# Two scatters of rows, and who signals the end of a matmul: matmul or drain

## The chip, the cores and the metric

The kernel runs on one core of a Trainium2 chip. The metric is the time of one execution on the device in microseconds (us). The core's engines are PE (TensorE, matmuls), DVE (VectorE), ACT (ScalarE), POOL (GpSimd) and SP (SyncE, which here only issues transfers). Each runs its own list of instructions in order; they meet at semaphores, which one instruction increments when it ends and another waits for.

## What is computed

Two layers over x of 16 x 256 x 128. Layer 0 multiplies a gated linear attention ("gla", a recurrence over chunks of 64 tokens with 4 heads) by the silu of a mixture of 8 experts; layer 1 multiplies a causal softmax attention with 16 heads by the silu of a mixture of 16 experts. Each token goes to its 2 best experts.

```python
xn = _layernorm(x)
s = _L0_attn_ref(xn, ...)            # gated linear attention
g = _silu(_L0_ffn_ref(xn, ...))      # top 2 of 8 experts
x = x + s * g
xn = _layernorm(x)
s = _L1_attn_ref(xn, ...)            # causal softmax attention, 16 heads of 8
g = _silu(_L1_ffn_ref(xn, ...))      # top 2 of 16 experts
x = x + s * g
```

## The kernel before, in words

The 4096 tokens are 16 batches of 256. For each layer DVE works out (`route`) a slot for each of the 8192 pairs of token and expert; POOL then sends the normalised rows to their slots in DRAM (the scatter); SP reads the sorted rows back in groups of 512, PE runs them through the experts (`ffn0` with 18 groups, `ffn1` with 20), and POOL stores the results with indirect transfers of its own (L1710).

One function, `walk`, fixes the order in which all engines write their programs. The parts that matter here:

- Layer 0: after `route(0)` come six turns t = 1 to 6. In each, POOL issues about a sixth of 64 indirect transfers of 128 rows (`scatter(0, t - 1, 6)`, L1694), and all engines do `gla(t, 0)`, `gla(t, 1)`, `gla(t, 2)`, one turn of the attention's software pipeline: gates (L430), keys times values (L481), turned keys (L456), scores (L469), values (L447), outputs (L495, L502), queries and keys (L441), projection (L516). Between its transfers POOL does two small steps of each turn: `output_gates` (L1730), which waits for ACT, and `chunk_ends` (L1724), which waits for ACT's exponentials; ACT's next exponentials wait for `chunk_ends`. Then `ffn0_begin` turns the first group of rows (L557), and the next turn of gla follows with the experts between its parts.
- Layer 1: after `route(1)` come seven turns in which POOL issues its 64 transfers with nothing between them but four small copies (L1690), while PE, ACT and DVE do 18 steps of the softmax attention ("mha", five steps to a batch of 256 tokens: 3.6 batches), and ACT and DVE also convert a piece of the expert weights (`mf`, L870 and L1353) in each turn. Then `ffn1_begin` turns the first group (L557 again), which needs the scatter done.

In an mha step `s1_four` makes four banks of scores (L679, closed by L682), which DVE reduces to maxima (L1580); `s2_four` makes four banks of scores turned the other way (L702, L706, closed by L709), of which ACT takes exponentials (L1110); `weigh` (L721, L723) multiplies by the values, `outputs_turned` (L748) and `heads_out` (L734) turn the results, and `queries_keys1` (L656) makes the next batch's queries and keys. PE hands out eight PSUM banks in a ring: a bank comes free when the engine that reads it has signalled.

In each of these steps the last matmul of a group carries the semaphore update for the reader, as `i.then_inc(qk.sem, 1)`; in `s1_four` and `s2_four` each of the four closing matmuls carries one. On PE `scatter` does nothing; it is only a point in the walk. The names `scattering`, `ended`, `scatter` and `begin` in the change are PE's alone.

Of the kernel before, what the change touches and what calls it, by code (L numbers as in the profile page):

```python
# [51 lines left out]
def build(nc, A, out):  # L52
    with ExitStack() as ctx:
# [26 lines left out]
        xnT = sb(4096)  # L80
# [262 lines left out]
        def _(eng):  # L343
# [10 lines left out]

            mm = partial(eng.matmul, start=True, stop=True, skip_group_check=True)

            def expert_logits(l, g):
                h, E = due(l, LOGITS, g), EXPERTS[l]
                if h is not None:
                    u = 8 * l + h  # L360
                    b = bank(("logits", u), l_moved.at(u))
                    eng.wait_ge(*n_moved.at(u))
                    if h == 0:
                        eng.wait_ge(*ld[f"rw{l}"].at(0))
                    for k in range(4):
                        t = 4 * h + k
                        i = mm(b[:, E * k:E * k + E], xnT[:, 128 * t:128 * t + 128], rw[l])  # L367
                    i.then_inc(logits.sem, 1)
                    if l == 0:
                        b = bank(("silu", h), silu_done.at(h))  # L370
                        if h == 0:
                            eng.wait_ge(*ld["wvg"].at(0))
                        mm(b[:, :], Wvg[:, 128:256], xnT[:, 512 * h:512 * h + 512]).then_inc(silu.sem, 1)

            def normed_turned(l, g):
                h = due(l, TURN, g)
                if h is not None:
                    u = 8 * l + h
                    b = bank(("norm", u), n_moved.at(u))
                    eng.wait_ge(*normed.at(u))  # L380
                    if u == 0:
                        eng.wait_ge(*ld["cst"].at(0))
                    for k in range(4):
                        i = eng.transpose(b[:, 128 * k:128 * k + 128], xn[:, 4 * h + k, :], ident)
                    i.then_inc(n_turned.sem, 1)

# [9 lines left out]
            def route(l):  # L396
                N, O = 64 * EXPERTS[l], one_hot[:, 0:64 * EXPERTS[l]]
                nh = N // 2
                eng.wait_ge(*chosen[l].at(1))
                eng.wait_ge(*set_dve.at(0, 3))  # L400
                for n, lhs in enumerate((trib, onesb)):
                    for i in range(2):
                        b = bank(("count", l, n, i), counts.at(l, 2 * n + i))
                        mm(b[:, 0:nh], lhs, O[:, nh * i:nh * i + nh]).then_inc(counted.sem, 1)
                if l == 1:
                    b = bank(("table", l), routed[l].at(0, 22))
                    eng.wait_ge(*routed[l].at(0, 21))
                    eng.wait_ge(*ld["phase"].at(0))
                    for c in range(2):
                        i = mm(b[:, 80 * c:80 * c + 80], phe[0:16, 128 * c:128 * c + 128], RS[l]["oh"][0:16, :])  # L410
                    i.then_inc(tabled.sem, 1)


            def gate_in(b):
                k = bank(("gate1", b), gate1_lo.at(b))
                if b == 0:
                    eng.wait_ge(*ld["gk1"].at(0))
                mm(k[0:80, 0:256], Wgk1, xnT[:, 256 * b:256 * b + 256]).then_inc(gate1.sem, 1)

            def gate_out(b):  # L420
                G = g1T[b % 2]
                eng.wait_ge(*gate1_lo.at(b))
                if b == 0:
                    eng.wait_ge(*set_dve.at(0, 3))
                for hp, k in enumerate(gate_banks):
                    if b > 0:
                        eng.wait_ge(*decay.at(b - 1, hp))
                    for h in range(2):
                        hh = 2 * hp + h
                        i = mm(k[:, 256 * h:256 * h + 256], Wgk2b[0:82, 128 * hh:128 * hh + 128], G[0:82, :])  # L430
                    i.then_inc(gate2.sem, 1)
# [12 lines left out]
            def values(b):  # L444
                k = bank(("v", b), v_moved.at(b))
                for u in range(2):
                    i = mm(k[:, 128 * u:128 * u + 128], xnT[:, 256 * b + 128 * u:256 * b + 128 * u + 128], Wvg[:, 0:128])  # L447
                i.then_inc(vv.sem, 1)

            def keys_turned(b, u):  # L450
# [4 lines left out]
                for h in range(4):  # L455
                    i = eng.transpose(k[:, 128 * h:128 * h + 128], k4[:, h, 128 * u:128 * u + 128], ident)  # L456
                i.then_inc(kt.sem, 1)

            def scores(b):
# [10 lines left out]
                i.then_inc(att.sem, 1)  # L470

            def key_values(b):
# [9 lines left out]
                i.then_inc(kv.sem, 1)  # L482

            def outputs(b):
# [12 lines left out]
                for n in range(1, 4):  # L497
# [5 lines left out]
                    if n > 1:  # L503
                        i.then_inc(o_mm.sem, 1)

            def output_means(b):
                eng.wait_ge(*o_sq.at(b))
                mm(o_banks[0][:, 256:512], means, osq[b % 2]).then_inc(o_mean.sem, 1)

            def project(b):  # L510
# [4 lines left out]
                for u in range(2):  # L515
                    i = mm(k[:, 128 * u:128 * u + 128], oy[b % 2][:, 128 * u:128 * u + 128], Wo)  # L516
                i.then_inc(wo_mm.sem, 1)

# [33 lines left out]
            def turn(l, g):  # L552
# [3 lines left out]
                for j in range(4):  # L556
                    i = eng.transpose(k[:, 128 * j:128 * j + 128], xsb[:, 129 * j:129 * j + 128], ident)  # L557
                i.then_inc(turned[l].sem, 1)
                if g == 0:
# [11 lines left out]
            def expert_up(l, g, j):  # L571
# [17 lines left out]
                for c in range(4):  # L589
# [6 lines left out]
                    if l == 0:  # L596
                        i = mm(o, b1r[:, 128 * c:128 * c + 128], b1s[:, bass.DynSlice(v * 128, 128)], start=False)  # L597
                i.then_inc(up[l].sem, 1)

# [46 lines left out]
            def queries_keys1(b, half):  # L646

                for n in (2 * half, 2 * half + 1):
# [8 lines left out]
                    j.then_inc(m_qk.sem, 1)  # L657

            def values1(b):
# [4 lines left out]
                for u in range(2):  # L664
                    i = mm(k[:, 128 * u:128 * u + 128], xnT[:, 256 * b + 128 * u:256 * b + 128 * u + 128], Wv)
                i.then_inc(m_v.sem, 1)

            def s1_four(b, n):
# [11 lines left out]
                for i, k in four:  # L680
                    kv_ = k[:, :].rearrange("p (n c) -> p n c", c=w)
                    mm(kv_[:, :, w - 128:w], identb, bc(negb, 1, [128, len(gs), 128]), start=False).then_inc(m_s1.sem, 1)  # L682

            def maxima_turned(b):
                k = bank(("neg", b), m_neg_moved.at(b))
                eng.wait_ge(*m_max.at(b))
                for u in range(2):
                    i = eng.transpose(k[:, :].bitcast(BF16)[:, 128 * u:128 * u + 128], negM[b % 2][:, u, :], identb)
                i.then_inc(m_neg.sem, 1)

            def s2_four(b, n):
# [15 lines left out]
                for i, k in four:  # L707
                    kv_ = k[:, :].rearrange("p (n c) -> p n c", c=w)
                    mm(kv_[:, :, 0:128], identb, bc(negtb, 1, [128, len(gs), 128]), start=False).then_inc(m_s2.sem, 1)  # L709

            def weigh(b, z):
# [6 lines left out]
                for m in range(2):  # L718
# [3 lines left out]
                    for i in range(4):  # L722
                        j = mm(k[32 * i:32 * i + 32, 256 * m + 128:256 * m + 256], V[:, 1, 4 * g + i, :], PT[1][:, i, g, :], start=False)  # L723
                j.then_inc(m_pv.sem, 1)

            def outputs_turned(b):
                for u in range(2):
# [7 lines left out]
                    i.then_inc(m_ot.sem, 1)  # L735

            def heads_out(b):
                k = bank(("yt", b), m_yt_moved.at(b))
                eng.wait_ge(*m_y.at(b))
                for u in range(2):  # L740
                    i = eng.transpose(k[:, 128 * u:128 * u + 128], yt[:, 128 * u:128 * u + 128], ident)
                i.then_inc(m_yt.sem, 1)

            def project1(b):
                k = bank(("proj", b), s1_done.at(b))
                eng.wait_ge(*m_yt_moved.at(b))
                for u in range(2):
                    i = mm(k[:, 128 * u:128 * u + 128], yT[:, 128 * u:128 * u + 128], Wproj)  # L748
                i.then_inc(m_proj.sem, 1)

# [1205 lines left out]
```

## Time and profile before

| | us |
|---|---|
| median of 3 runs | 1166.89 (1165.84 to 1169.87) |
| the profiled execution | 1174.48 |
| its span, first to last instruction | 1172.5 |
| PE busy | 794.8 (68%) |
| DVE busy | 646.4 (55%) |
| ACT busy | 625.9 (53%) |
| POOL busy | 479.5 (41%) |
| mean granted TensorE clock | 0.83 |

The profile page gives the busy time of each engine, the span in 40 slices, and the chain of waits: the work that ended last, followed back from the end through whatever released each step. "issue" is time in which an engine waited for nothing that the profile shows; "another core or an unknown queue", and "remote" in the table of waits, is a wait for which the profile finds no event that ended it at that time. A matmul's end is modelled; its start is recorded.

### The profile page before, as it was taken

Reading aid. Unit: us, or ns where it says so; the run is one execution under the profiler, and the core shown is the slowest. Engines: PE = TensorE matmul, PEld = TensorE weight load, DVE = VectorE, ACT = ScalarE, POOL = GpSimd, SP = SyncE. Lnnn points to the kernel's source line nnn. Section 1 sums busy time; section 2 is a strip of 40 time slices with the busy share of each in tenths; the row PEclk is TensorE's granted clock in tenths of the full one; section 3 lists DMA queues with packets and bytes.
Section 4 is the critical chain, followed back from the end, with each engine's and each line's share of the span. In section 5 each row is a group of like instructions: output and inputs, shape, how many; then the busy total and the mean of one; then the engine's idle time right before and its main releaser. Section 6 shows DMA issues by size and latency. Waiting matters only on the chain.

```text
span 1172.5 us, 23626 instructions
## 1 busy us (share of the span) xinstructions
PE 794.8 (68%) x8916; PEld 620.2 (53%) x8916; DVE 646.4 (55%) x1112; ACT 625.9 (53%) x1093; POOL 479.5 (41%) x486
## 2 busy tenths in 40 slices
PE   5735668999999882477821028777988788788610
PEld 3424557888888762254610015455656566666510
DVE  7574336766765233977670016755656647465355
ACT  4433336768775311464500025667668778687722
POOL 3067542233432444520037730004346646555635
PEclk9667869999999997677955559989889999899855
DMA  9511111011011113300013111201001111010052
GB/s 325 190 45 55 52 39 45 21 34 34 29 34 33 47 47 111 78 1 2 1 29 147 52 43 37 73 19 29 20 28 38 35 31 38 28 38 29 19 152 72
DMA packets 62366, 63.92 MB, mean 55 GB/s; under 512 B 7378, under 2 KB 52322, under 8 KB 62132
## 3 DMA queue, kind: packets, MB, share of 16 engines
q1 hardware_dynamic: 53300, 43.99, 12.8%
q0 software_dynamic: 8960, 18.43, 4.8%
q8 instruction: 77, 1.26, 0.5%
q14 instruction: 29, 0.24, 0.1%
HBM read 31.84 MB, written 30.55 MB: 53 GB/s over the span
## 4 chain that ended last, share of the span: by engine, by line
PE 38%; DVE 19%; ACT 13%; another core or an unknown queue 11%; issue 10%; POOL 6%; DMA 2%; SPq 0%; POOLq 0%; ACTq 0%; DVEq 0%
PE bank L441 5%; POOL ys L1710 4%; PE bank L656 3%; ACT arena L1110 3%; PE bank L593 3%; DVE arena L1580 2%; ACT L804 2%; PE bank L595 2%; PE bank L607 2%; PE bank L481 2%; PE bank L594 2%; PE bank L721 2%; PE bank L621 1%; PE bank L367 1%
## 5 line engine op out<-in xcount | busy, mean ns | idle before, releaser
L1710 POOL DMA_INDIRECT ys<-arena x152 | 169.8, 1117 | 203.3 <-DVE arena L1472 86.0
L1110 ACT ACTIVATE arena<-bank 128x512 f32<-128x512 f32 x192 | 99.3, 600 | 137.2 <-remote 92.1
L1694 POOL DMA_INDIRECT xs<-arena x128 | 128.4, 1003 | 62.4 <-issue 36.5
L593 PE MATMUL bank<-arena 128*128 128x128 bf16 x608 | 139.2, 236 | 19.4 <-DVE arena L1453 7.4
L595 PE MATMUL bank<-arena 128*128 128x128 bf16 x608 | 138.8, 235 | 3.8 <-issue 3.8
L1580 DVE TENSOR_REDUCE arena<-bank 128x2 bf16<-128x512 f32 (+1 forms) x192 | 119.2, 683 | 40.2 <-remote 26.2
L594 PE MATMUL bank<-arena 128*128 128x128 bf16 x608 | 136.7, 232 | 3.9 <-issue 3.9
L804 ACT ACT_TABLE_LOAD x70 | 89.8, 1283 | 1.2
L593 PEld LDWEIGHTS bank<-arena 128*128 x608 | 63.3, 104 | 37.5 <-issue 28.5
L441 PE MATMUL bank<-arena 128*128 128x256 f32 x256 | 69.1, 424 | 18.4 <-DVE arena L1359 17.2
L679 PE MATMUL bank<-arena 32*128 32x256 bf16 (+1 forms) x512 | 22.3, 263 | 86.7 <-ACT arena L1110 61.2
L1750 POOL TENSOR_TENSOR arena<-arena 128x1024 f32<-128x1024 f32 x20 | 47.0, 2351 | 71.3 <-ACT arena L1025 71.2
L1500 DVE TENSOR_SCALAR arena<-bank 128x512 f32<-128x512 f32 x40 | 27.6, 691 | 85.5 <-ACT arena L1011 85.3
L1568 DVE SCALAR_TENSOR_TENSOR arena<-arena,bank 128x512 bf16<-128x512 bf16 x64 | 46.2, 746 | 47.4 <-ACT arena L1083 46.1
L441 PEld LDWEIGHTS bank<-arena 128*128 128x128 f32 x256 | 53.2, 216 | 29.5 <-DVE arena L1359 18.0
L595 PEld LDWEIGHTS bank<-arena 128*128 x608 | 62.8, 103 | 9.1 <-issue 4.3
L656 PE MATMUL bank<-arena 128*128 128x256 f32 x256 | 66.0, 404 | 0.7 <-issue 0.7
L594 PEld LDWEIGHTS bank<-arena 128*128 x608 | 63.8, 105 | 4.8 <-issue 4.4
L597 PE MATMUL bank<-arena 128*128 x288 | 63.3, 220 | 3.1 <-issue 3.0
L679 PEld LDWEIGHTS bank<-arena 32*128 32x128 bf16 x512 | 9.5, 96 | 97.1 <-issue 75.9
L1462 DVE SCALAR_TENSOR_TENSOR arena<-arena,bank 128x512 f32<-128x512 f32 x36 | 24.7, 690 | 54.8 <-ACT arena L987 35.0
L656 PEld LDWEIGHTS bank<-arena 128*128 128x128 f32 x256 | 49.5, 204 | 8.8 <-issue 2.5
(213 smaller groups left out, 2034.5 us busy)
## 6 DMA issues: line engine op xcount, KB each, us to landing
xs<-arena SPq DMA_DIRECT2D x19, 516.0 KB, 7.7
arena<-xs SPq DMA_DIRECT2D x38, 258.0 KB, 2.8
arena<-ys SPq DMA_DIRECT2D x32, 256.0 KB, 5.2
arena<-in_MF SPq DMA_DIRECT2D x8, 512.0 KB
ys<-arena POOLq DMA_INDIRECT x152
arena<-in_x SPq DMA_DIRECT2D x8, 256.0 KB, 5.6
arena<-in_W SPq DMA_DIRECT2D x8, 256.0 KB
xs<-arena POOLq DMA_INDIRECT x128
```

The source lines that it names most:

```text
L441: i = mm(k[:, 256 * h:256 * h + 256], (Wq, Wk)[n // 2][:, 128 * hh:128 * hh + 128], xnT[:, cols])
L593: mm(o, hi, b[:, 0, c4], stop=False)
L594: mm(o, hi, b[:, 1, c4], start=False, stop=False)
L595: i = mm(o, lo, b[:, 0, c4], start=False, stop=(l == 1))
L597: i = mm(o, b1r[:, 128 * c:128 * c + 128], b1s[:, bass.DynSlice(v * 128, 128)], start=False)
L656: j = mm(k[:, 256 * z:256 * z + 256], Wqk[:, c:c + 128], xnT[:, 256 * b:256 * b + 256])
L804: eng.preload_act_table_set(name)
L1110: act(PT[kt_][:, i, gs[0]:gs[0] + len(gs), :], bank_of["s2", b, n, i][:, :].rearrange("p (g q) -> p g q", q=w), ACT.Exp, scale=8 ** -0.5). ...
L1580: red(negM[b % 2][:, u, 32 * i + gs[0]:32 * i + gs[0] + len(gs)], kv_, op=ALU.max, negate=True).then_inc(m_max.sem, 1)
L1694: eng.indirect_dma_start(xs[l][:, :], bass.IndirectOffsetOnAxis(ap=slot_i[l][:, m:m + 1], axis=0), xrow[:, t, :], None).then_inc(rows_move ...
L1710: eng.indirect_dma_start(ys[l][:, :], bass.IndirectOffsetOnAxis(ap=yid[g % 4][:, j:j + 1], axis=0), y[:, 128 * j:128 * j + 128], None).the ...
L1750: tt(T, T, U, ALU.mult).then_inc(f1_h.sem, 1)
```

## The change

Between the first `scatter` of a layer and the begin of its experts, PE puts a drain behind the group, without a wait of its own, and lets the drain increment the semaphore. In `s1_four` and `s2_four` a drain stands behind the second and behind the fourth closing matmul and adds two each time. Outside the two stretches each update stays on its matmul. No matmul, transfer or wait is added, removed or moved. The built program has 167 such drains: 81 in the turns of layer 0 (24 behind L441, 12 behind L430, 10 behind L456, 8 behind L502), 86 in the 18 steps of layer 1 (24 in `s1_four`, 24 in `s2_four`, 12 behind L656). They carry what 215 matmuls carried.

```diff
+            scattering = [False]
+
+            def ended(i, s, n=1):
+                if scattering[0]:
+                    eng.drain().then_inc(s.sem, n)
+                else:
+                    i.then_inc(s.sem, n)
+
+            def scatter(l, i, n):
+                scattering[0] = True
+
+            def begin(l):
+                scattering[0] = False
+                turn(l, 0)
...
             def queries_keys(b):
...
                         i = mm(k[:, 256 * h:256 * h + 256], (Wq, Wk)[n // 2][:, 128 * hh:128 * hh + 128], xnT[:, cols])
-                    i.then_inc(qk.sem, 1)
+                    ended(i, qk)
...
             def s1_four(b, n):
...
-                    mm(kv_[:, :, w - 128:w], identb, bc(negb, 1, [128, len(gs), 128]), start=False).then_inc(m_s1.sem, 1)
+                    j = mm(kv_[:, :, w - 128:w], identb, bc(negb, 1, [128, len(gs), 128]), start=False)
+                    if not scattering[0]:
+                        j.then_inc(m_s1.sem, 1)
+                    elif i % 2:
+                        ended(j, m_s1, 2)
...
             def s2_four(b, n):
...
-                    mm(kv_[:, :, 0:128], identb, bc(negtb, 1, [128, len(gs), 128]), start=False).then_inc(m_s2.sem, 1)
+                    j = mm(kv_[:, :, 0:128], identb, bc(negtb, 1, [128, len(gs), 128]), start=False)
+                    if not scattering[0]:
+                        j.then_inc(m_s2.sem, 1)
+                    elif i % 2:
+                        ended(j, m_s2, 2)
...
-            walk({"setup": nothing, "set_gates": nothing, "set_later": nothing, "norm": norm, "norm_end": norm_end, "gla": gla, "route": route, "scatter": nothing, "w1": nothing,
-                  "ffn0_begin": lambda: turn(0, 0), "ffn0": ffn0, "mha_begin": all_banks, "join": nothing, "last_join": nothing, "mha1": mha1, "mha2": mha2,
-                  "mf": nothing, "ffn1_begin": lambda: turn(1, 0), "ffn1": ffn1, "end": nothing})
+            walk({"setup": nothing, "set_gates": nothing, "set_later": nothing, "norm": norm, "norm_end": norm_end, "gla": gla, "route": route, "scatter": scatter, "w1": nothing,
+                  "ffn0_begin": lambda: begin(0), "ffn0": ffn0, "mha_begin": all_banks, "join": nothing, "last_join": nothing, "mha1": mha1, "mha2": mha2,
+                  "mf": nothing, "ffn1_begin": lambda: begin(1), "ffn1": ffn1, "end": nothing})
```

The other groups of the two stretches (gates, values, turned keys, scores, outputs, projections, maxima) are changed as `queries_keys` is.

## Rows read from the trace of the kernel before

**Rows 1.** The page's span in 40 slices of 29.3 us.
```profile
PE   5735668999999882477821028777988788788610
POOL 3067542233432444520037730004346646555635
PEclk9667869999999997677955559989889999899855
```
**Rows 2.** The chain of waits in order of time: start, us, what.
```profile
86.24 3.97 another core or an unknown queue
105.83 4.34 another core or an unknown queue
137.55 11.67 another core or an unknown queue
...
610.92 7.41 another core or an unknown queue
622.28 67.49 another core or an unknown queue
...
868.71 5.25 another core or an unknown queue
```
**Rows 3.** Timeline, layer 1: start, us, engine, line, operation, count, [idle before, releaser].
```profile
621.90 0.38 ACT L1125 ACTIVATE arena<-bank 128x256 f32<-128x256 f32 x1 [0.57 <-remote]
622.43 0.61 PE L702 MATMUL bank<-arena 32*128 32x256 bf16 x8 [1.75 <-ACT arena L1125]
623.40 1.03 PE L709 MATMUL bank<-arena 128*128 128x256 bf16 x4
635.20 0.69 DVE L1580 TENSOR_REDUCE arena<-bank 128x2 bf16<-128x512 f32 x1 [20.53 <-remote]
635.95 1.22 PE L748 MATMUL bank<-arena 128*128 128x128 f32 x4 [11.51 <-issue]
686.29 0.96 POOL L1694 DMA_INDIRECT xs<-arena  x1 [0.30 <-issue]
689.80 0.60 ACT L1110 ACTIVATE arena<-bank 128x512 f32<-128x512 f32 x1 [67.51 <-remote]
```
**Rows 4.** Timeline, layer 0, the same columns.
```profile
64.46 1.28 POOL L1694 DMA_INDIRECT xs<-arena  x1 [12.43 <-DVE arena L1313]
118.62 5.21 PE L441 MATMUL bank<-arena 128*128 128x256 f32 x14
123.02 0.96 POOL L1694 DMA_INDIRECT xs<-arena  x1 [0.30 <-issue]
125.65 0.45 ACT L930 ACTIVATE arena<-bank 128x128 f32<-128x128 f32 x2 [11.30 <-remote]
170.53 0.96 POOL L1694 DMA_INDIRECT xs<-arena  x1 [0.30 <-issue]
```
**Rows 5.** Timeline of PE, layer 0: where turns 3, 6 and 7 start.
```profile
94.88 0.60 PE L430 MATMUL bank<-arena 82*128 82x256 bf16 x4
...
178.35 0.60 PE L430 MATMUL bank<-arena 82*128 82x256 bf16 x4
193.44 0.60 PE L557 MATMUL bank<-arena 128*128 128x128 f32 x4
194.31 0.60 PE L430 MATMUL bank<-arena 82*128 82x256 bf16 x4
```
**Rows 6.** Timeline, layer 1: first matmul and last group of the 18 steps.
```profile
609.37 0.29 PE L679 MATMUL bank<-arena 32*128 32x128 bf16 x3
753.30 8.44 SPq L1824 DMA_DIRECT2D arena<-xs  x3
757.14 0.19 POOL L1703 COPY arena<-arena 128x4 int32<-128x4 int32 x1 [69.89 <-DMA arena<-xs]
760.75 0.60 PE L557 MATMUL bank<-arena 128*128 128x128 f32 x4
```
**Rows 7.** The chain of waits, layer 1: one batch's L656 to the next's.
```profile
721.74 1.88 PE bank L656 x8
742.21 1.88 PE bank L656 x8
```
**Rows 8.** One group of matmuls by duration (min/median/max).
```profile
L656 PE MATMUL bank<-arena x256: 379/379/767, 483.9 to 1047.3; 128*128 128x256 f32 x128
```
**Rows 9.** Timeline: PE's eight L656 behind each other, unstarved.
```profile
746.87 1.99 PE L656 MATMUL bank<-arena 128*128 128x256 f32 x8
```

More of the change, by code:

```diff
@@ L367, in expert_logits @@
                         i = mm(b[:, E * k:E * k + E], xnT[:, 128 * t:128 * t + 128], rw[l])
-                    i.then_inc(logits.sem, 1)
+                    ended(i, logits)
                     if l == 0:
@@ L384, in normed_turned @@
                         i = eng.transpose(b[:, 128 * k:128 * k + 128], xn[:, 4 * h + k, :], ident)
-                    i.then_inc(n_turned.sem, 1)
+                    ended(i, n_turned)
             def norm(l, g):
@@ L410, in route @@
                         i = mm(b[:, 80 * c:80 * c + 80], phe[0:16, 128 * c:128 * c + 128], RS[l]["oh"][0:16, :])
-                    i.then_inc(tabled.sem, 1)
+                    ended(i, tabled)
             def gate_in(b):
@@ L417, in gate_in @@
                     eng.wait_ge(*ld["gk1"].at(0))
-                mm(k[0:80, 0:256], Wgk1, xnT[:, 256 * b:256 * b + 256]).then_inc(gate1.sem, 1)
+                ended(mm(k[0:80, 0:256], Wgk1, xnT[:, 256 * b:256 * b + 256]), gate1)
             def gate_out(b):
@@ L430, in gate_out @@
                         i = mm(k[:, 256 * h:256 * h + 256], Wgk2b[0:82, 128 * hh:128 * hh + 128], G[0:82, :])
-                    i.then_inc(gate2.sem, 1)
+                    ended(i, gate2)
             def queries_keys(b):
@@ L447, in values @@
                     i = mm(k[:, 128 * u:128 * u + 128], xnT[:, 256 * b + 128 * u:256 * b + 128 * u + 128], Wvg[:, 0:128])
-                i.then_inc(vv.sem, 1)
+                ended(i, vv)
             def keys_turned(b, u):
@@ L456, in keys_turned @@
                     i = eng.transpose(k[:, 128 * h:128 * h + 128], k4[:, h, 128 * u:128 * u + 128], ident)
-                i.then_inc(kt.sem, 1)
+                ended(i, kt)
             def scores(b):
@@ L469, in scores @@
                             i = mm(k[64 * c:64 * c + 64, o:o + 64], k4[:, h, n], q4[:, h, n])
-                i.then_inc(att.sem, 1)
+                ended(i, att)
             def key_values(b):
@@ L481, in key_values @@
                         i = mm(k[:, o:o + 32 * z], KT[:, 512 * u + 128 * h:512 * u + 128 * h + 128], v[:, u, h, 0:z, :].rearrange("p c d -> p (c d)"))
-                i.then_inc(kv.sem, 1)
+                ended(i, kv)
             def outputs(b):
@@ L516, in project @@
                     i = mm(k[:, 128 * u:128 * u + 128], oy[b % 2][:, 128 * u:128 * u + 128], Wo)
-                i.then_inc(wo_mm.sem, 1)
+                ended(i, wo_mm)
             def gla(t, part):
@@ L557, in turn @@
                     i = eng.transpose(k[:, 128 * j:128 * j + 128], xsb[:, 129 * j:129 * j + 128], ident)
-                i.then_inc(turned[l].sem, 1)
+                ended(i, turned[l])
                 if g == 0:
@@ L597, in expert_up @@
                         i = mm(o, b1r[:, 128 * c:128 * c + 128], b1s[:, bass.DynSlice(v * 128, 128)], start=False)
-                i.then_inc(up[l].sem, 1)
+                ended(i, up[l])
             def down0(g):
@@ L656, in queries_keys1 @@
                         j = mm(k[:, 256 * z:256 * z + 256], Wqk[:, c:c + 128], xnT[:, 256 * b:256 * b + 256])
-                    j.then_inc(m_qk.sem, 1)
+                    ended(j, m_qk)
             def values1(b):
@@ L665, in values1 @@
                     i = mm(k[:, 128 * u:128 * u + 128], xnT[:, 256 * b + 128 * u:256 * b + 128 * u + 128], Wv)
-                i.then_inc(m_v.sem, 1)
+                ended(i, m_v)
             def s1_four(b, n):
@@ L688, in maxima_turned @@
                     i = eng.transpose(k[:, :].bitcast(BF16)[:, 128 * u:128 * u + 128], negM[b % 2][:, u, :], identb)
-                i.then_inc(m_neg.sem, 1)
+                ended(i, m_neg)
             def s2_four(b, n):
@@ L723, in weigh @@
                         j = mm(k[32 * i:32 * i + 32, 256 * m + 128:256 * m + 256], V[:, 1, 4 * g + i, :], PT[1][:, i, g, :], start=False)
-                j.then_inc(m_pv.sem, 1)
+                ended(j, m_pv)
             def outputs_turned(b):
@@ L734, in outputs_turned @@
                         i = eng.transpose(k[:, 128 * g:128 * g + 128], OT[g // 2][:, o:o + 128], ident)
-                    i.then_inc(m_ot.sem, 1)
+                    ended(i, m_ot)
             def heads_out(b):
@@ L741, in heads_out @@
                     i = eng.transpose(k[:, 128 * u:128 * u + 128], yt[:, 128 * u:128 * u + 128], ident)
-                i.then_inc(m_yt.sem, 1)
+                ended(i, m_yt)
             def project1(b):
@@ L748, in project1 @@
                     i = mm(k[:, 128 * u:128 * u + 128], yT[:, 128 * u:128 * u + 128], Wproj)
-                i.then_inc(m_proj.sem, 1)
+                ended(i, m_proj)
             def mha1(t, n):
```

8 lines of the change are left out of this document (4 added, 4 removed).

## Prediction, made before the changed kernel ran

> **What bounds the kernel now.** I read the span in slices first. PE's busy share falls to 1 and 0 in the slices around 620 to 680 us, where POOL's stands at 7, and PE's clock shows 5 tenths, its lower level of 1.2 GHz [rows 1]. No engine that computes is loaded there, so something is waited for. The chain of waits says what kind of thing: 67.49 us in one piece, and 7.41 us just before, put down to "another core or an unknown queue", and smaller pieces of 3.97, 4.34 and 11.67 us between 86 and 149 us [rows 2]. A kernel on one core has no other core, so I went to the timeline.
>
> In layer 1 PE starts the four closing matmuls L709 at 623.40. ACT's L1110, which reads their banks, starts at 689.80. The last of POOL's indirect transfers starts at 686.29. DVE's L1580 gets its first bank at 635.20 though PE went on to later work at 622.43 [rows 3]. So matmuls are done and their readers do not learn of it. It is not the matmuls that stand still: PE runs L748 at 635.95, behind L709 in its order. And it is not semaphores in general: ACT's L1125 ends at 622.28 and PE's L702 starts 0.15 us later; DVE's L1580 ends at 635.89 and PE's L748 starts 0.06 us later [rows 3]. Only what matmuls increment is late, and it comes when POOL stops. Layer 0 shows the same at a smaller size. PE starts the last 14 of its L441 at 118.62, behind the outputs; ACT's L930, which reads those outputs, starts at 125.65 after 11.30 us idle, just after POOL's run of transfers ended (the last starts at 123.02) [rows 4]. There the stall is shorter because POOL itself waits for ACT once in each turn and thereby stops.
>
> **The change part by part.** It does one thing in two places: 215 updates leave matmuls, 167 drains take them. Its worth hangs on a question that no row of before answers, since no drain stands inside that program: does the update of a drain get through while POOL runs its transfers? I take it that it does, and give the other answer below as a rival. For it speaks that what is late is tied to the path that matmuls use: PE's waits and starts are prompt in the same microseconds, and so are the updates of two other engines [rows 3].
>
> The Trainium skill, "Perfetto Trace Analysis", sections on the sequencer-only and the tensor engine instruction, says that a matmul's update is pushed once PSUM has acknowledged its bytes, and that of an instruction like a drain by the sequencer. The rows fit a late first kind; no run here yet shows the second. By that page the two paths differ, which is the forecast's side; if they meet again behind it, it is the rival's.
>
> Gain in layer 1. The stretch from the first L679 to L557 of `ffn1_begin` is 760.75 - 609.37 = 151.4 us [rows 6]. Undisturbed, a batch of five steps takes 742.21 - 721.74 = 20.5 us [rows 7], pieces of `mf` included. 18 steps are 3.6 batches, 73.8 us. So 77.6 us of the stretch are the stall, and that is the most that can go.
>
> Cost of a drain. It holds PE's next instruction until the group has ended. Eight L656 take 1.99 us from the first start to the last end [rows 9] and one takes 0.379 [rows 8], so starts lie (1.99 - 0.379) / 7 = 0.23 us apart, and the overlap lost is 0.379 - 0.23 = 0.15 us. To start again once released takes up to the 0.15 us seen between ACT's end at 622.28 and PE at 622.43 [rows 3]. That gives 0.15 to 0.30 us for each drain; I take 0.25, nearer the upper end because the next weights can hardly be loaded ahead across it. A drain may lie under a wait that PE has anyway, so nothing is the lowest charge; a gain from drains themselves I exclude, since they only hold back. I charge all of it to the path, as the chain in such batches runs mostly through PE: 86 x 0.25 = 21.5 us in layer 1 (bounds 0 and 25.8).
>
> The Trainium skill, "TensorE: Matmul & The Clock Gate", section "Single matmul latency", speaks against the change: an isolated matmul shows a fixed part of some 166 ns warm that a stream of them hides. 167 times that is an estimate of 28 us over the kernel, where 167 x 0.25 is 42; by the page the time would be about 14 us lower than mine. "PSUM — Partial Sum Buffer", section "Engine vs sequencer instructions", says that a drain waits for the engine to go fully idle, so a drain is a sound carrier; no run here shows that yet.
>
> So L557 would come at 609.4 + 73.8 + 21.5 = 704.7 instead of 760.75, a gain of 56 us. What is late next: the scatter itself. Its last transfer starts at 686.29 [rows 3] and rows read back took 757.14 - 753.30 = 3.8 us [rows 6], so the rows could be there at about 694 and do not decide; they become the floor if drains cost nothing (gain at most 67).
>
> Gain in layer 0. Turn 7 starts (L430) at 194.31, turn 3 at 94.88 [rows 5], and the latter is already late by the 3.97 us piece [rows 2], so it would start at 90.9. The turn from 178.35 to 194.31 ran without a transfer of POOL's and took 16.0 us [rows 5]. Four such turns are 64 us, with 54 drains (81 / 6 a turn) at 0.25 us, 13.5: turn 7 at 168.4, a gain of 25.9 us. The floor is POOL: from 64.46 [rows 4] 64 transfers at 1.27 us (0.96 and the 0.30 between) are 81.3 us, its last now starts at 170.53, and with five turns' own steps at some 3 us each it would be done at 161, so it does not decide by a few us. That floor is near, and a part of this gain may go to it.
>
> Sum: 56.0 + 25.9 = 82 us. Against the profiled execution 1174.48 - 82 = 1092.5. The median lies 7.6 us below that execution, so 1085.
>
> What the change doesn't touch: POOL's stores in bursts of four during the experts show such pieces too (5.25 us at 868.71 [rows 2]) and stay.
>
> **The rivals.**
>
> Full relief and cheap drains: as above, with drains under waits. Gain 67 + 31 (floor at 161 and some us for turn 7, so 163) = 98, time 1069. It is the lower end of the forecast's own range; I go a little further, to 1062, for matmuls at the higher clock where PE's level stood at 5 tenths [rows 1].
>
> Part of the relief: drains get through late, or only in one layer. Layer 0 alone would give 1141, layer 1 alone 1111; a delay of 0.5 us for each of 167 drains on top of the forecast, 1168. So 1100 to 1163.
>
> No relief, no loss: what starves matmuls' updates starves drains' too, or the wait of readers is simply for POOL to stop. Then PE, idle for most of both stretches, hides the drains. Time 1163 to 1170. For it: PE is one engine with perhaps one way out for both kinds.
>
> Slower, by one mechanism: a drain does not end while an update is held up, and so PE, which now runs ahead of a stuck update (14 L441 at 118.62 behind outputs not yet reported [rows 4]), stops at each. It decides in layer 0, if the drain is released only when POOL pauses. Then a turn is POOL's run and the whole turn behind each other: 10.7 x 1.27 + 16.0 = 29.6 us, against (194.31 - 94.88 - 16.0) / 3 = 27.8 now, 5 us over three turns; in layer 1 the steps would all fall behind the scatter, 687.3 + 73.8 + 21.5 = 782.6 against 760.75, 22 us. Up to 27 us, 1194; with the drains half hidden some 1180. Against it: PE's plain matmuls and waits move freely during the stall [rows 3].
>
> **How the numbers follow.** Full relief, at my price or cheaper (1062 to 1100): 0.47, the likeliest. Part (1100 to 1163): 0.15. Neither: 0.15. Slower: 0.23, about half of it under 1180. The range 1062 to 1180 leaves out the rest of that half and the far low end, some 0.15 in all. The forecast's own range is 1062 to 1100. Within 0.3% (3.5 us) is what a measurement of this kernel can't tell from no change: faster 0.62, same 0.15, slower 0.23.
>
> **What would show it.** Right: the pieces of 67.49 and 11.67 us are gone from the chain; L1110 starts under 1 us behind its L709 while POOL still issues; L557 of layer 1 stands near 700 and turn 7 of layer 0 near 168, with POOL's transfers still 1.27 us apart. The price of a drain is read from L656 and L441: the gap between one group of four and the next. Wrong: L1110 still waits until POOL's last transfer (no relief); L441 no longer runs ahead and all steps start behind the scatter (slower); or the stall shrinks and turns of 16 us become 20 or more, then the drains cost more than 0.3 us each.

## The result, and the profile after

| | before | after |
|---|---|---|
| median, us | 1166.37 (4 runs, 1161.17 to 1169.87) | 1208.76 (4 runs, 1205.07 to 1210.91) |
| profiled execution's span, us | 1172.5 | 1203.2 |

The ratio is 1.0364, 95% interval 1.0314 to 1.0413: the change makes the kernel 3.6% slower, 42 us where 82 us had been forecast the other way. A second set, run later, gave 1.0305 (1.0252 to 1.0358).

The page of after, in 40 slices of 30.1 us, answers to [rows 1]:

```profile
PE   4644766999999885267922028877788878788710
POOL 3077242142343345620017740002336546646635
PEclk9656667999999998587955559979989999999865
```

The hole is still there: from 632 to 692 us PE stands at 2 and 0 while POOL stands at 7. What is new is that the profile can now name what is waited for. The drain is an instruction with a start and an end of its own. The line of the program that holds it, by instructions (engine, operation, count: min/median/max ns, first and last start):

```profile
L360 PEldq DRAIN  x167: 273/1008/49300, 54.8 to 795.0; - x167
```

The unit is ns: one drain takes 49.3 us. The table of waits puts what stood as "remote" in before on it:

```profile
ACT arena L1132 <- PEq L360: 103.7, 13, 66.9
```

(L1132 is the exponential that was L1110; lines behind the change moved by 22, and PE's by up to 18: L709 is now L727, L656 L670, L430 L444, L502 L516, L682 L696, L557 L571.) The timeline of layer 1, to be held against [rows 3]:

```profile
655.46 0.60 PE L696 MATMUL bank<-arena 128*128 128x256 bf16 x2 [11.24 <-issue]
661.59 0.61 PE L727 MATMUL bank<-arena 128*128 128x256 bf16 x2
710.03 1.08 ACT L1132 ACTIVATE arena<-bank 128x512 f32<-128x512 f32 x2 [66.86 <-PEq L360]
710.06 0.60 PE L727 MATMUL bank<-arena 128*128 128x256 bf16 x2 [47.86 <-issue]
```

Two of the four closing matmuls start at 661.59. The drain behind them starts at 660.7, before them, as PE's sequencer comes to it while they are still queued, and takes 49.3 us, to 710.0; it ends just after POOL's last transfer, which starts at 707.35, and only then do the other two matmuls start. ACT starts within 0.1 us of the drain's end, so the drain's update is prompt and it is its end that is late. In before all four ran at once and PE went on to later work. So a drain is held as the matmul's own update was, and it holds PE as well.

In neither kernel is the hold complete while POOL runs. In before the four banks of the L682 that start at 619.64 reach DVE one after the other, in order, in the middle of POOL's run: the first at 635.20 [rows 3], the second and the fourth at

```profile
638.00 0.69 DVE L1580 TENSOR_REDUCE arena<-bank 128x2 bf16<-128x512 f32 x1 [2.11 <-remote]
642.90 0.69 DVE L1580 TENSOR_REDUCE arena<-bank 128x2 bf16<-128x512 f32 x1 [2.80 <-remote]
```

The L709 of 623.40, next in order, waits until 689.80. In after, too, drains end in mid-run: PE goes on at 655.46, after 11.24 us, and at 660.61.

In layer 0 of after the turns start at

```profile
135.24 0.85 PE L444 MATMUL bank<-arena 82*128 82x256 bf16 x4 [0.23 <-issue]
166.61 0.85 PE L444 MATMUL bank<-arena 82*128 82x256 bf16 x4 [0.23 <-issue]
197.64 0.85 PE L444 MATMUL bank<-arena 82*128 82x256 bf16 x4 [0.23 <-issue]
214.35 0.63 PE L571 MATMUL bank<-arena 128*128 128x128 f32 x4 [0.23 <-issue]
215.45 0.60 PE L444 MATMUL bank<-arena 82*128 82x256 bf16 x4
```

that is 31 us apart with transfers and 17.8 without, against 25.2, 26.5 and 16.0 in before (its turns 4 to 7 start at 126.69, 151.87, 178.35 and 194.31). Turn 3 grew from 31.8 to 37.7 us. The first L571 (214.35 against 193.44 [rows 5]) and the last group of layer 1 (796.20 against 760.75 [rows 6]) give the account of the profiled executions: +20.9 us by the first group of layer 0, +35.4 by the first group of layer 1 (so 14.5 more), +30.7 at the end.

### The profile page after: what moved, and what is told of

It is laid out like the page before. It is cut to its first block, busy times and chain, and to the rows that moved or that the text cites. A ratio compares the mean times of both kernels' runs of the same rounds, so it can differ in the third digit from the quotient of the medians.

```text
span 1203.2 us, 23793 instructions
## 1 busy us (share of the span) xinstructions
PE 811.5 (67%) x8916; PEld 608.6 (51%) x8916; DVE 647.8 (54%) x1112; ACT 627.4 (52%) x1093; POOL 480.9 (40%) x486
## 4 chain that ended last, share of the span: by engine, by line
PE 30%; issue 24%; DVE 15%; ACT 11%; PEld 6%; POOL 6%; PEldq 4%; DMA 2%; another core or an unknown queue 1%; SPq 0%; POOLq 0%; ACTq 0%; DVEq 0%
POOL ys L1732 4%; PEldq L360 3%; PE bank L455 3%; PE bank L607 3%; PE bank L670 2%; ACT arena L1132 2%; DVE arena L1602 2%; ACT L826 2%; PE bank L609 2%; PE bank L621 2%; PE bank L608 2%; PE bank L495 1%; PEld bank L455 1%; PE bank L635 1%
## 5 line engine op out<-in xcount | busy, mean ns | idle before, releaser
L1132 ACT ACTIVATE arena<-bank 128x512 f32<-128x512 f32 x192 | 99.3, 599 | 147.1 <-PEq L360 103.7
L455 PE MATMUL bank<-arena 128*128 128x256 f32 x256 | 76.0, 445 | 16.4 <-DVE arena L1381 14.3
L727 PE MATMUL bank<-arena 128*128 128x256 bf16 (+1 forms) x192 | 44.9, 353 | 53.9 <-issue 53.1
L670 PE MATMUL bank<-arena 128*128 128x256 f32 x256 | 66.7, 403 | 2.4 <-issue 1.6
L670 PEld LDWEIGHTS bank<-arena 128*128 128x128 f32 x256 | 48.2, 200 | 12.9 <-issue 5.5
L727 PEld LDWEIGHTS bank<-arena 128*128 128x128 bf16 x192 | 14.9, 103 | 74.3 <-issue 70.0
```

The source lines that it names most:

```text
L727: j = mm(kv_[:, :, 0:128], identb, bc(negtb, 1, [128, len(gs), 128]), start=False)
L1132: act(PT[kt_][:, i, gs[0]:gs[0] + len(gs), :], bank_of["s2", b, n, i][:, :].rearrange("p (g q) -> p g q", q=w), ACT.Exp, scale=8 ** -0.5). ...
```

## The experiments

All are edits of the kernel before, except where drains are named. They ran on several chips, and this turned out to matter: the median of the kernel before was 1166 to 1186 us on some and 1035 to 1037 us on two others. I call the first holding chips and the second free chips, for a reason that follows. Ratios are always to before in the same set on the same chip; they can differ by up to 0.4% from the quotient of the two medians.

### Drains in one layer alone

```diff
             def scatter(l, i, n):
-                scattering[0] = True
+                scattering[0] = l == 0
```

and with `l == 1`.

> The changed kernel with its drains kept in layer 0's six turns alone. Theory H (a matmul is not retired while POOL issues its transfers; a drain waits for that and holds PE's queue, so PE can no longer run ahead): the loss of layer 0 as the two traces show it, 21 us at L571's place of layer 0 (214.35 against 193.44), so 1187 us. Rival R (the whole loss is the price of a drain, some 0.25 us each, alike in both layers): 81 of 167 drains, 42 x 81 / 167 = 20 us, 1187 too in time, but then the turns without transfers are as slow as the others; H wants 5 to 6 us lost in each turn with transfers and under 2 us in turn 6 to 7.

> The changed kernel with its drains kept in layer 1's eighteen steps alone. Theory H: during the scatter PE is already stopped, so drains can cost nothing there, and cost only what they take in the steps that run after the scatter; the two traces give 14.5 us for the stretch up to the first group, less some that comes back: 1177 us. Rival R (price alone, alike everywhere): 22 us, 1189.

This was a free chip. Before took 1036.96 us. Drains in layer 0 gave 1040.96 (ratio 1.0049, 1.0030 to 1.0069), in layer 1 1047.53 (1.0102, 1.0084 to 1.0119). Neither theory had expected a chip on which before is 130 us faster. In the profile of the second, whose layer 0 is that of before, no wait on "remote" is left, and two of its turns, with the same run of transfers on POOL, are

```profile
132.26 0.60 PE L444 MATMUL bank<-arena 82*128 82x256 bf16 x4
149.12 0.60 PE L444 MATMUL bank<-arena 82*128 82x256 bf16 x4
166.52 0.60 PE L444 MATMUL bank<-arena 82*128 82x256 bf16 x4
```

16.9 and 17.4 us, where before on the holding chip has 25.2 and 26.5. (The turn in front of them takes 27.5 us here too, DVE waiting 9.93 of them for L1752, a step that POOL does between its transfers.) On such a chip the matmuls' updates are prompt while POOL issues, and drains cost only their price. The price can be read from batches of layer 1, the kernel with drains there first, then the one without (first L670 of a batch to that of the next):

```profile
614.97 2.31 PE L670 MATMUL bank<-arena 128*128 128x256 f32 x8 [0.38 <-issue]
638.64 2.31 PE L670 MATMUL bank<-arena 128*128 128x256 f32 x8 [0.23 <-issue]
```

```profile
604.30 1.99 PE L670 MATMUL bank<-arena 128*128 128x256 f32 x8
625.32 1.99 PE L670 MATMUL bank<-arena 128*128 128x256 f32 x8
```

23.7 us against 21.0: 2.7 us for 24 drains, 0.11 us each.

The first of the two again, on a holding chip:

> Drains in layer 0 alone, again, for a chip where before takes about 1167 us. Theory H there: 20 us lost, 1.7%, 5 to 6 us in each turn that has transfers. Rival R (price alone): 4 us as on the first chip, 0.4%. Where before takes 1037 us: 0.5% again.

1197.60 us against 1185.77, ratio 1.0109 (1.0036 to 1.0182): 12 us, three times the 4.0 us of the free chip, though less than the 20 us that theory H forecast. The interval reaches down to about 4 us, the price alone, so the times by themselves do not decide. The profile does: the first group stands at 213.61 as in after (214.35), and the longest of the 81 drains takes 10.8 us, where the longest on the free chip takes 2.3. So the price alone does not explain it; some of the 20 us is given back later.

### The changed kernel again

> The changed kernel once more. On the chip of the last four runs the kernel before took 1037 us and no matmul's update was late, where it took 1166 us in the runs shown. Theory C (the late retirement of matmuls is there on some chips and not on others): where before takes about 1037, the change costs the sum of its parts there, 4.0 us for layer 0 and 10.6 us for layer 1: 1.0 to 1.8%, no drain longer than 3 us; where before takes about 1166, it costs 3.1 to 4.1% again and drains of 40 us and more are there. Rival D (the first four differ by something in their text and not by the chip): before takes 1166 again beside a changed kernel of 1037 or the like, or the cost doesn't follow the time of before.

Before 1170.74 us, the changed kernel 1208.55, ratio 1.0305 (1.0252 to 1.0358); its longest drain took 48.6 us. Theory C held at both ends: the loss goes with the time of before. Rival D is out. The chip of the first set is not known, and each of the others but this one was used in one set only; here before took 1170.74 us in this set and 1185.77 in the next, so whether the difference belongs to the chip, to the core or to the moment is not shown; I go on saying chip.

### What starts the hold: POOL's transfers or the loads of weights

In before updates were prompt for the first 8 us of layer 1's scatter (the L709 of 613.35 is the first late one, its reader starting at 618.35), and SP issued 3 MB of loads at 612 us. The kernel `nosp` holds these loads until the scatter has ended.

```diff
                 else:
                     eng.wait_ge(*routed[1].at(0))
+                    for i in range(16):
+                        eng.wait_ge(*last_scatter(1, i))
                 dma(rbuf[c % 2], A["MF"][:, 1024 * c:1024 * c + 1024]).then_inc(ld_mf[c % 2].sem, 16)
...
                 mha(20 + 18 * t // 7, 20 + 18 * (t + 1) // 7)
+            for t in range(8):
                 do["mf"](t)
-            do["mf"](7)
```

`quarter1` issues 16 of the 64 transfers of layer 1. Most rows that its experts read are then zeros, and its last join reads layer 0's results in place of layer 1's.

```diff
-            return rows_moved[i].sem, 64 * l + 64
+            return rows_moved[i].sem, (64, 80)[l]
...
                 for m in range(64 * i // n, 64 * (i + 1) // n):
+                    if l == 1 and m >= 16:
+                        continue
...
-                    src = ys[l][4096 * k + 512 * g:4096 * k + 512 * g + 512, :].rearrange("(t p) d -> p t d", p=128)
+                    src = ys[0][4096 * k + 512 * g:4096 * k + 512 * g + 512, :].rearrange("(t p) d -> p t d", p=128)
```

> The kernel before, with layer 1's loads of expert weights (in_MF, in_DN) held until the scatter has ended, and the eight conversions put behind the eighteen steps. In before, matmuls' updates were prompt for the first 9 us of the scatter and late from 614 us, just after those loads were issued at 612. Theory S (the loads set the stall off): no update later than 1 us during the scatter, L1110 of step 20 and on run freely, steps done with the scatter at about 690, first group not before the conversions, some 15 us on, so L1 stretch shorter by 50 us. Theory P (POOL's transfers alone do it): ACT's exponentials wait until POOL stops, as before, and the kernel is 10 to 20 us slower, by the conversions now standing alone.

> The kernel before with only the first 16 of layer 1's 64 scatter transfers, so most rows that the experts read are zeros; the last join reads layer 0's results in place of layer 1's. Theory P: the stall lasts as long as POOL issues, 20 us instead of 81; 48 x 1.27 = 61 us go, about 1106, in the timed runs as in the profiled one. Theory S: the stall starts with the loads and has its own length; under 20 us go.

On the free chip they gave 1061.69 (1.0244, 1.0213 to 1.0276) and 1031.48 (0.9928, 0.9892 to 0.9964). The first, 25 us where theory P had 10 to 20, are loads and conversions that now stand behind the scatter: in its profile SP reads the sorted rows only behind the last of these loads, and the first group of layer 1 waits 41.52 us for them. The second says that 48 transfers less are worth 5.5 us there. On a holding chip:

> Layer 1's weight loads held until the scatter has ended, conversions behind the steps, for a chip where before takes about 1167 us. Theory P: ACT's exponentials still wait for POOL's end; 25 us slower than before, as on the first chip (1062 against 1037). Theory S: updates prompt throughout the scatter; 77 us of stall gone, 25 added: 1115.

> Only the first 16 of layer 1's 64 transfers (most rows are zeros, the last join reads layer 0's results), for a chip where before takes about 1167 us. Theory P (POOL's transfers do it, for as long as it issues them): 48 x 1.27 = 61 us go, 1106, in timed and profiled runs alike. Theory S (the loads at 612 us set it off, with a length of its own): under 20 us go. On the first chip, where nothing stalled, it took 1031 against 1037.

`nosp` took 1197.74 against 1185.77 (1.0121, 1.0083 to 1.0158), and its chain of waits shows, with no load in flight,

```profile
613.51 9.65 another core or an unknown queue
627.79 70.44 another core or an unknown queue
```

So the loads do not start the hold; theory S is out. As in before, the first late update is that of the L709 that starts behind the sixth transfer. The last held one came at 698.22, 9.4 us after POOL's last transfer had started at 688.87, against 3.5 us in before; the held loads had started at 691.22, and whether they delay a release was not tested. The whole came out 13 us better than expected of theory P. A likely reason is that the first loads here run beside steps that the hold has pushed back (the first group waits 23.05 us for its rows, not 41.52); it was not tested. `quarter1` took 1115.95 (0.9411, 0.9324 to 0.9498): 70 us gone for 48 transfers, 1.45 us each where theory P had 1.27, against 5.5 us in all on the free chip. On a holding chip a transfer costs the kernel more than the 1.27 us that it takes POOL, on a free one a tenth of it. The timed and the profiled executions say the same, so it is no artefact of profiling.

### Pauses for landing

POOL waits after every four transfers until these have landed, in layer 1 (`paused1`), in both layers (`p4_both`), or after every eight in both (`p8_both`).

```diff
+                    if l == 1 and m and m % 4 == 0:
+                        for j in range(m - 4, m):
+                            eng.wait_ge(rows_moved[j % 16].sem, 64 + 16 * (j // 16 + 1))
                     if m >= 16 or l:
                         eng.wait_ge(rows_moved[m % 16].sem, 64 * l + 16 * (m // 16))
```

> The kernel before, but in layer 1 POOL waits after every four transfers until these have landed: 15 pauses of some 2 us, so its run of 81 us becomes about 110 us. Theory P with release in every pause: matmuls' updates come at each pause, every 7 us or so, and steps get on during the scatter; of the 18 steps' chain of about 4 handovers a step some 15 are done by then; the end moves little, within 10 us of before. Theory Q (a pause must be long, or the outstanding transfers must end, before anything is retired): no steps done during the scatter, 29 us slower. Where before takes 1037 us: steps run freely, first group waits for the longer scatter, 15 to 20 us slower.

1151.87 us against 1185.77, 0.9696 (0.9622 to 0.9770): a longer scatter and a faster kernel. The steps were done and PE then waited for the rows:

```profile
740.30 1.09 PE L557 MATMUL bank<-arena 128*128 128x128 f32 x4 [30.50 <-DMA arena<-xs]
```

The timeline shows more than theory P asked for: PE ran on also while the four transfers of a run were issued. Hence theory T, that the hold builds up over an unbroken run.

> The kernel before with a pause in both scatters after every eight transfers, until these have landed (some 2.3 us each, 7 pauses in a scatter). The run with four transfers between pauses showed PE running freely even while the four were issued, and in before PE was prompt for the first 8 or 9 transfers of layer 1. Theory T (late retirement builds up only over a long unbroken run of transfers, and a pause resets it): at eight PE is free nearly throughout; the scatter of layer 1 ends 18 us later than in before, at about 705, steps by then; first group at 710 to 715: 45 us gained, and 10 to 20 in layer 0: 5% faster where before takes 1170 to 1186. Theory P (late in proportion to the time in which POOL issues): 3% as with four, or less. Where before takes 1037: 0 to 1% slower.

> The same with four transfers between pauses, in both layers. Layer 1 as measured, 34 us gained; in layer 0 a turn of 26 us has 13.5 us of transfers, 2 to 3 pauses add 6 us to POOL's part and free PE: turns of about 20 us, 20 us gained; some 4.5% faster where before takes 1170 to 1186, 1 to 2% slower where it takes 1037, since the longer scatter then sets the end.

Both on a holding chip: after eight 1114.61 us (0.9550, 0.9478 to 0.9622), after four 1136.06 (0.9726, 0.9641 to 0.9810, less than the 4.5% expected), before 1171.69. Fewer pauses did better, since most cost POOL 2.0 to 2.4 us, a few up to 7.9, and with four the scatter decides again (PE waited 34.89 us for the rows at 726.27). With eight, layer 0's first group came at 171.50 in place of 193.44 [rows 5]. Some late updates were left there, in layer 1 up to 8.2 us, so a run of eight is already long.

### Pauses without landing

```diff
+                    if m and m % 4 == 0:
+                        for j in range(5):
+                            eng.memset(yid[3], 0).then_inc(spun.sem, 1)
+                            eng.wait_ge(spun.sem, 5 * (15 * l + m // 4 - 1) + j + 1)
```

(`spin4` has it in layer 1 alone; before the first of layer 1 POOL also awaits layer 0's stores, which are long done.)

> The kernel before, and in layer 1 POOL fills the time after every four transfers with five small memsets, each awaited, some 2.4 us in all, and does not wait for the transfers. Theory U (it is enough that POOL issues no transfer for 2 us): as the run with pauses for landing in layer 1 alone, 3% faster where before takes 1170 to 1186, first group near 740. Theory V (the transfers in flight must land): no or little gain, the stall goes on, first group at 775 or later.

1108.19 us against 1171.69, 0.9475 (0.9375 to 0.9576), first group at 706.09, more than the 3% expected. Theory U: after a run of four it is enough that POOL issues nothing for 1.4 us (the memsets took less than the 2.4 us planned); the transfers in flight need not land.

> The kernel before with five small awaited memsets on POOL (1.4 us without a transfer) after every four transfers, in both scatters. Theory T (late retirement builds up over an unbroken run of transfers and a short pause undoes it): 60 us gained in layer 1 as in the run with layer 1 alone, and turns of layer 0 of 17 to 19 us in place of 26, 20 to 25 us more: 7% faster where before takes 1170 to 1186. Where it takes 1037: within 0.5%, as POOL's scatter of layer 1 grows by 20 us but was not the last to end.

> The same after every eight transfers. Theory T with a reset at each pause: the pauses for landing after eight gave 4.5%; these are shorter by 1 us each, so about 5.5% faster, with waits of up to 8 us for matmuls' updates left. Where before takes 1037: within 0.3%.

> The changed kernel, drains and all, with the pauses of spin4_both. Theory H (the loss is PE's queue held behind unretired matmuls, plus a price of some 0.1 us a drain): with the holding gone the drains cost what they cost where before takes 1037, 15 us against spin4_both; no drain longer than some 6 us. Rival R (drains are costly on such a chip for themselves): 35 to 42 us against spin4_both.

These three fell on a free chip (before 1035.00): 1069.77 (1.0320, 1.0284 to 1.0356), 1052.49 (1.0153, 1.0117 to 1.0190) and, the changed kernel with pauses, 1071.51 (1.0352, 1.0315 to 1.0389). I had expected pauses to be free there. They are not. In layer 1 the scatter already sets the start of the experts without them, as the profile of `d_l0` on a free chip shows, and with `spin4_both` PE waited 27.67 us for its rows at 686.72:

```profile
653.93 1.09 PE L571 MATMUL bank<-arena 128*128 128x128 f32 x4 [8.88 <-DMA arena<-xs]
```

About half of the 35 us is lost in layer 0 already, where the first group stands at 179.66 against 162.25 in `nosp`, whose layer 0 is that of before. The drains on top cost 1.7 us. The same three on a holding chip (before 1185.57):

> Pauses of 1.4 us after every four transfers in both scatters, where before takes 1167 to 1186. Layer 1 alone gave 5.3% with them; layer 0's turns fall from 26 us towards the 17 to 20 us that the same pauses allow, 20 us more: 7% faster, 1090. If instead layer 0 was not held by runs of transfers: 5%, 1110. Where before takes 1037: 3.2% slower again.

> After every eight: 5.5% faster (1105) by pauses for landing after eight, which gave 4.5%; 7% if the shorter pause is as good as the long one. Where before takes 1037: 1.5% slower again.

> The changed kernel with those pauses. Theory H (held queue plus a small price): against spin4_both_b the drains cost 2 to 15 us, as they cost where nothing is held, in place of 38 to 42. Rival R (costly for themselves on such a chip): 35 us or more.

`spin4_both` took 1108.14 (0.9369, 0.9327 to 0.9411), `spin8_both` 1140.59 (0.9646, 0.9599 to 0.9694), the changed kernel with pauses 1137.91 (0.9586, 0.9542 to 0.9631). The first two gained less than the 7% and the 5.5 to 7% expected. The timeline of the first shows the release itself:

```profile
639.83 1.99 PE L657 MATMUL bank<-arena 128*128 128x256 f32 x8
642.11 0.96 POOL L1702 DMA_INDIRECT xs<-arena  x1 [0.30 <-issue]
643.07 0.75 POOL L1698 MEMSET arena<- 128x4 int32 x5
644.13 0.69 DVE L1589 COPY arena<-bank 128x512 f32<-128x512 f32 x1 [5.67 <-remote]
644.19 1.09 ACT L1084 ACTIVATE arena<-bank 128x512 bf16<-128x512 f32 x2 [4.72 <-remote]
```

POOL ends a run of four at 643.07, DVE and ACT get what they waited 4.7 to 5.7 us for at 644.13 and 644.19, and POOL goes on at 644.43.

`spin8_both_b` shows the limit: after runs of eight the same pause does not always release. DVE's L1589 reads what matmuls that start at 632.93 had closed, and starts at 643.08 after 17.56 us idle; POOL had issued no transfer from 636.96 to 638.59, and was issuing again when the update came. ACT waits 17.21 us, until 664.76, across the pause from 659.89 to 661.50. With pauses for landing after eight the longest such wait of layer 1 was 8.2 us. So whether the landing matters is settled for runs of four only.

The drains of the changed kernel with pauses:

```profile
L361 PEldq DRAIN  x167: 275/1088/4402, 57.0 to 732.7; - x167
```

The longest fell from 49.3 to 4.4 us; on the free chip it is 2.5. Yet drains still cost 29.8 us against `spin4_both_b`, between the 2 to 15 of theory H and the 35 of rival R: neither forecast held. In the profiles 21.6 us are lost by the first group of layer 0 (194.89 against 173.32) and 19.7 more by that of layer 1 (733.66 against 692.41). My reading is that the pauses shorten the holds but do not remove them, and that a drain makes PE wait out each that is left, 167 times instead of where a reader happens to need it. The waits on the drain fit this, but how the 29.8 us divide between holds and price was not measured apart.

## Why the prediction was wrong, point by point

**The reading of before was right in the main.** PE's matmuls were late for their readers while POOL issued, and the stall was about 78 us in layer 1. `quarter1_b` (70 us back) and `spin4` (some 62 us) bear it out, and on a free chip no such wait is left. That a late update "comes when POOL stops" was too simple: [rows 3] itself has DVE's first bank at 635.20, some 50 us before POOL's end.

**The step that failed** is the one that was called open and then taken: "does the update of a drain get through while POOL runs its transfers? I take it that it does". It does not: a drain takes up to 49.3 us. I had concluded from PE going on to later matmuls that only the carrying of updates was late. What the drains show is that later matmuls may start in such a stretch but a drain may not end. The simplest reading is that the earlier matmuls were not retired, that is, not yet counted as finished; that banks come free one by one and in order fits it. A drain without an update, which would tell this from a drain that is kept from handing over its update, was not run. The rows of before could not tell the two apart, since a matmul's end is modelled and only its start recorded; I had the sentence for it and did not use it against my own theory. With this step fell both gains, 56.0 and 25.9 us.

The Trainium skill, "PSUM — Partial Sum Buffer", section "Engine vs sequencer instructions", had the rule that I should have weighed: a drain waits for the engine to go fully idle. The trace is in line with it if the two matmuls were unfinished: the drain ends 48.4 us after they start, where the profile gives them 0.61 us. I had cited it only for soundness.

I had also leaned on the Trainium skill, "Perfetto Trace Analysis", section "Sequencer-only Instruction (DRAIN, etc)", by which the sequencer pushes a drain's update. In the trace that last step takes under 0.1 us, from the drain's end to ACT's start; it did not help, as the end came late.

**The rival that came true** is the slower one, as a mechanism: PE stops at each held drain. It was given 0.23 and priced at up to 1194 where 1208.8 was measured, so also the range, to 1180, was too short: I had cut it inside a rival whose own upper price lay above. Its larger error was in layer 0, priced at 5 us where 20.9 were lost. Turns of 29.6 us were forecast against 27.8 before; over turns 3 to 5 the trace has 33.4 on average (97.55 to 197.64), 16.6 us more in three turns, and 4.3 us more lie before turn 3 and behind turn 5. In layer 1 "steps would all fall behind the scatter, 22 us" was 14.5, as in before nearly all of them were behind it already: from PE's start after the stall, 690.54, to the first group it took 70.2 of the 73.8 us. Of the 14.5, some 11 are the price of drains in steps behind the scatter (3.6 batches at 3.0 us each, see below).

Timed medians lost 42 us and the profiled executions 30.7. The other 11 are no stretch of the kernel: the profiled execution of before lay 8.1 us above its median and that of after 3.7 below.

**The price of a drain** was put at 0.25 us, bounds 0.15 to 0.30. Measured 0.11 (free chip) and, in after behind the scatter, 747.18 to 770.70 for a batch, 23.5 us against 20.5 [rows 7], 0.13. It was mis-sized by two; that part of it lies under waits that PE has anyway is likely and was not measured. By the latency of a single matmul, in the Trainium skill, "TensorE: Matmul & The Clock Gate", section "Single matmul latency", the estimate was 0.17; the measurements are under that too.

**The floors.** "The scatter itself is late next" was right: with pauses after every four transfers the rows decide in layer 1, and on the free chip they do without any (8.88 us of waiting in `d_l0`).

## What to carry to other kernels

Where a wait ends on a matmul whose start is long past, do not ask only how its signal is carried; ask whether the matmul is finished, and try one drain at that place, since its duration in the profile tells. On a drain hangs everything behind it, so here it could not cure a slow completion. The cure was at the cause: to break POOL's long run of indirect transfers by 1.4 us after every four made the kernel 6.3% faster on a chip that holds, and 3.2% slower on one that does not, so measure before on more than one chip before such a change is kept.

## What the runs showed of the hardware that I had not expected

- While POOL issues indirect transfers back to back (one in 1.27 us), the end of matmuls of the same core is reported late on some chips; in before a reader waited up to 67.5 us. On two others it is not: before took 1035 to 1037 us there against 1166 to 1186, and the waits on "remote" are absent from the profiles. Why is open, and whether it stays with a chip as well.
- The long holds need a long run. In before and in `nosp_b` the first late update of layer 1 came after six or seven transfers. With runs of four and pauses of 1.4 us, in which the transfers in flight need not land, the longest wait for an update in layer 1's scatter was 7.1 us (`spin4_both_b`); with runs of eight and the same pauses it was 17.6 us, across a pause (`spin8_both_b`).
- What is held comes in order and in part during the run: four banks at 635.20 to 642.90 in before, the next at 689.80.
- Two updates of ACT and DVE in the same microseconds were prompt, 0.15 and 0.06 us [rows 3]. By what path POOL's transfers and the completion of PE's matmuls meet was not found out.
